# Row numbers for the gathers of a graph network: converted by GpSimd for each slot instead of by ScalarE for eight slots

## The chip, the cores and the metric

The kernel runs on one core of a Trainium2 chip. The metric is device time in microseconds (us) of one execution, as the median of several executions without the profiler. The engines are called as in the profile: PE is TensorE (PEld its weight loads), DVE is VectorE, ACT is ScalarE, POOL is GpSimd and SP is SyncE. POOL issues the indirect DMAs that gather rows; ACT and SP issue plain DMAs.

## The reference

Three rounds of message passing over a graph with 6250 nodes of 512 features (float32) and 100,000 edges that come sorted by target:

```python
x = _layernorm(x + gcn(x, edges) + t_emb @ Wt + bt)        # L = 0
h = relu(mean_of_sources(x) @ Wl1.T + x @ Wr1.T + b1)      # L = 1
y = mean_of_sources(h) @ Wl2.T + h @ Wr2.T + b2            # L = 2
out = _layernorm(x + y)
```

In each round the source rows of all edges are gathered and summed by target. The targets are drawn as 6250·u² with u even between 0 and 1, so targets with low numbers have many edges and those with high numbers few.

## The kernel before, in words

Edges are cut into groups of 256 (CH = 2 gathers of 128 rows). A group fills one of SLOTS = 8 slots of the tile `raw`; eight groups are a block, and each of the three layers (L = 0, 1, 2) goes over the same 42 blocks, so 336 slots and 672 gathers a layer, 1008 slots and 2016 gathers in all.

**GpSimd** does nothing in the layers but these gathers (`gather`, lines 549 to 561, called for two blocks by `two_blocks`, 563 to 566, in the loop of line 568). For each slot n it waits until PE has read the slot (`slot_read[n]`, line 554), counts `slot_claimed` (555) and issues two indirect DMAs (558), each of which takes 128 row numbers (int32, one column of `idx_ring`) and fetches 128 rows of 2 KB. Between two layers it waits until the table for the next one is stored (545, 547).

**The row numbers** lie as int16 in `idx_tab` and are wanted as int32. `idx_ring` holds the numbers of two blocks, 16 columns each. ACT converts them, a block at a time: `next_indices` (1021 to 1025) copies 128 x 16 numbers into one half of the ring and counts `idx_copied`. It does so for the first two blocks ahead of the layers (1032, 1033), and then at the end of each block of its own loop for the block after the next, once the last slot of its block has landed (1158, 1159). POOL waits for `idx_copied` once a block (551).

**PE** waits for a slot (`slot_full[n]`, 1423) and adds its rows to the sum of a window of 64 targets with a one-hot matrix (`add_chunk`, 1330); the first of these matmuls frees the slot before it (1425, 1428). Where a window of targets ends, PE does more (`window_end`, 1285): it closes the sum (1335), adds what belongs to the next window (1304), transposes the sum of a finished tile (1315) and multiplies it by a weight matrix (`weigh`, 1324). In L = 1 and L = 2 it also multiplies the nodes' own rows by a second matrix (`own_rows`, 1345; line 1341); a plan made at the start spreads these over the first part of the layer. **DVE** makes the one-hot matrices and adds up, **ACT** evacuates sums from PSUM.

The order on each engine is that of its own program; semaphores are all that joins them. POOL runs up to eight slots ahead of PE.

Of the kernel before, what the change touches and what calls it, by code (L numbers as in the profile page):

```python
# [5 lines left out]
def gnn_resnorm(nc, x, src, dst, t_emb, w0, b0, wt, bt, wl1t, wr1t, b1, wl2t, wr2t, b2, out):  # L6
    fp32, bf16 = mybir.dt.float32, mybir.dt.bfloat16
    i32, i16 = mybir.dt.int32, mybir.dt.int16
    ALU, ACT = mybir.AluOpType, mybir.ActivationFunctionType
# [14 lines left out]
    CH = 2  # L24
    GROUP = CH * P
    SLOTS = 8
# [57 lines left out]
    with ctx:  # L84
        def sb(name, shape, dt, scope=ctx):
            return scope.enter_context(nc.sbuf_tensor(name, shape, dt))
# [4 lines left out]
        def sem(name):  # L91
            return ctx.enter_context(nc.semaphore(name))
# [10 lines left out]
        idx_tab = sb("idx_tab", [P, (NBLK + 2) * SLOTS * CH], i16)  # L103
# [29 lines left out]
        idx_ring = sb("idx_ring", [P, 2 * SLOTS * CH], i32)  # L133
# [124 lines left out]
        S = {n: sem(n) for n in names}  # L258
        slot_full = [sem(f"slot_full{n}") for n in range(SLOTS)]
# [10 lines left out]
        def free_again(n, L, uses):  # L270

            return L * (n == SLOTS - 1) + 1 + uses
# [9 lines left out]
        def first_block(eng):  # L282

            eng.wait_ge(S["start_made"], 1)
            return eng.value_load(start_blk[0:1, 0:1], min_val=0, max_val=B0MAX)

        def each_block(eng, b0, L, part, step=1):

            begin = (NBLK - b0) * L
            with eng.Fori(begin & BLOCK_BITS, begin + (NBLK - b0), step) as i:  # L290
                part(i, nc.s_assert_within(i + (b0 - begin), 0, NBLK - 1,
                                           skip_runtime_bounds_check_because="the blocks from the first one on"))
# [18 lines left out]
        def own_loads(L):  # L311

            return (0, OWN0, OWN0 + T + 1, OWN0 + 2 * T + 3)[L]
# [166 lines left out]
        def _(pool):  # L480
# [54 lines left out]
            b0 = first_block(pool)  # L535
            pool.wait_ge(S["b0_all_ps"], 1)
            pool.wait_ge(S["ranges_made"], 1)
            pool.wait_ge(S["tabs_made"], 2)
            for L in range(NL):
                if L == 0:  # L540

                    pool.wait_ge(S["stage_stored0"], 16 * 4 * PAIRS)
                    pool.wait_ge(S["stage_stored1"], 16 * 3 * PAIRS)
                elif L == 1:
                    pool.wait_ge(S["x_stored"], 16 * T)
                else:
                    pool.wait_ge(S["h_stored"], 16 * (T + HID + LAG))

                def gather(i, half):

                    pool.wait_ge(S["idx_copied"], i + 1)
                    for n in range(SLOTS):

                        pool.wait_ge(slot_read[n], i + free_again(n, L, 0))
                        pool.sem_inc(S["slot_claimed"], 1)
                        for j in range(CH):
                            at = (half * SLOTS + n) * CH + j
                            nc.gpsimd.indirect_dma_start(  # L558
                                out=raw[:, n, j, :], out_offset=None, in_=tables[L][:, :],
                                in_offset=bass.IndirectOffsetOnAxis(ap=idx_ring[:, at:at + 1], axis=0),  # L560
                            ).then_inc(slot_full[n], 16)

                def two_blocks(i, b):

                    gather(i, 0)
                    gather(i + 1, 1)

                each_block(pool, b0, L, two_blocks, 2)

# [412 lines left out]
        def _(act):  # L982
            a = nc.scalar
# [23 lines left out]
            for n, (first, many) in enumerate(TWOS):  # L1007
                b = first // BT
# [7 lines left out]
            b0 = first_block(act)  # L1016
# [1 line left out]
                         ACT.Copy).then_inc(S["tabs_made"], 1)  # L1018
            act.wait_ge(S["tabs_made"], 3)

            def next_indices(to_half, of_block):

                a.activation(idx_ring[:, bass.ds(to_half * (SLOTS * CH), SLOTS * CH)],
                             idx_tab[:, bass.ds(of_block * (SLOTS * CH), SLOTS * CH)],
                             ACT.Copy).then_inc(S["idx_copied"], 1)

            def next_counts(t1):

                a.activation(cbuf[:, :], counts[:, :, :].rearrange("p t n -> p (t n)")[:, bass.ds(t1 * P - P, P)], ACT.Copy,
                             scale=1.0).then_inc(S["cbuf_ready"], 1)  # L1030

            for blk in range(2):
                next_indices(blk, b0 + blk)

            def take_counts(w, of):

                act.wait_ge(S["c_ready"], w + 1)
                of_nodes = of[:, 0:KEYS].rearrange("p (n h) -> p h n", n=NODE)
                a.activation(counts[:, 0:T - 1, bass.ds(w * NODE, NODE)], of_nodes[:, 1:T, :], ACT.Copy)
                a.activation(counts[:, T - 1:T, bass.ds(w * NODE, NODE)], of_nodes[:, 0:1, :],  # L1040
                             ACT.Copy).then_inc(S["c_taken"], 1)
# [6 lines left out]
            def first_counts():  # L1048

                act.wait_ge(S["c_taken"], DW + 2)  # L1050
                next_tile(1)

            def tile_ahead(done):

                act.wait_ge(S["dense_done"], done)
                next_tile(nc.s_assert_within(done + 1, 1, OWN0, skip_runtime_bounds_check_because="a tile or an empty one"))
# [60 lines left out]
            for L in range(NL):  # L1117

                if L == 1:
                    act.wait_ge(S["x_stored"], 16 * T)  # L1120
                elif L == 2:
                    act.wait_ge(S["h_stored"], 16 * (T + HID + LAG))
                if L > 0:
                    act.dma_start(selfbuf[:, :], rows32[L - 1][2 * P:3 * P, :]).then_inc(S["self_loaded"], 16)

                def counts_of_half(i, half):

                    def taken(i):

                        take_counts(i * 2 + half, (root_ps, dense_ps)[half])  # L1130
                        if half == 1:
                            with act.If(i > COUNT_BLOCKS - 2):
                                first_counts()
                            act.nop()

                    def ahead(d):

                        if half == 0:
                            tile_ahead(d * 2 + 1)
                        else:  # L1140
                            with act.If(d < DENSE_BLOCKS - 1):
                                tile_ahead(d * 2 + 2)
                            act.nop()

                    early_blocks(act, i, taken, ahead)

                def groups(i, b):

                    ends = halves_before(mybir.EngineType.Activation, b)
                    if L > 0:  # L1150
                        rounds = rooted_before(mybir.EngineType.Activation, b)
                    for half in range(2):
                        if L > 0:
                            each(act, rounds[half], rounds[half + 1], lambda r: own_rows(L, r), T)
                        else:
                            counts_of_half(i, half)
                        each(act, ends[half], ends[half + 1], lambda w1: window_end(L, w1))
                    act.wait_ge(slot_full[SLOTS - 1], i * (16 * CH) + 16 * CH)
                    next_indices(i & 1, b + 2)

                each_block(act, b0, L, groups)
                take_transposed(L, T)
                if L == 1:
                    act.wait_ge(S["root_ready"], T + 1)
                    act.dma_start(W[1][:, :, :], wr2t.rearrange("(k p) d -> p k d", p=P)).then_inc(S["wr_loaded"], 16)
                    act.wait_ge(S["root_added"], T + 1 + LAG)
                    act.dma_start(b_all[:, :], b2.rearrange("(a d) -> a d", a=1).to_broadcast([P, D])
                                  ).then_inc(S["b_loaded"], 16)
                    act.wait_ge(S["h_stored"], 16 * (1 + HID + LAG))
                    act.wait_ge(S["self_loaded"], 16 * own_loads(2))  # L1170
                    act.dma_start(selfbuf[:, :], rows32[1][P:2 * P, :]).then_inc(S["self_loaded"], 16)
                    next_counts(1)
                    rectify(L, T - 1)
                    rectify(L, T)
                    take_own(2)
                else:
                    deviation(L, T - 1)
                    deviation(L, T)
                    if L == 0:
                        act.wait_ge(S["dense_done"], OWN0)  # L1180
                        next_counts(1)
                        take_own(1)
# [284 lines left out]
```

## Time and profile before, and how to read them

| what | value |
|---|---|
| median of 3 runs without the profiler | 2886.89 us (2882.86 to 2890.46) |
| profiled execution: span from its first to its last instruction | 3459.0 us |
| profiled execution: time around the span | not shown by the page |
| mean granted TensorE clock in it | 0.902 of full speed |

One execution was traced; it took 572 us more than the median. A row such as "L558 POOL DMA_INDIRECT raw<-rows,idx_ring x1344 | 1277.9, 951 | 939.8 <-issue 498.3" says: line 558, engine POOL, operation, tile written and tiles read, 1344 instructions, together 1277.9 us busy, 951 ns for one; the engine sat idle 939.8 us just before them, and 498.3 us of that ended for no reason that the profile shows ("issue"). "remote" is a release whose source is not in the records. For an indirect DMA on POOL the row tells of the engine's own work, not of the arrival of the rows.

### The profile page before, as it was taken

What the parts mean: (1) busy time and instruction counts of PE and PEld (TensorE: products, weight loads), DVE (VectorE), ACT (ScalarE), POOL (GpSimd) and SP (SyncE); (2) the same over time, 40 slices, a digit from 0 to 9 for tenths busy, and PEclk for the clock granted to TensorE, in tenths of its full rate; (3) what the DMA queues carried; (4) which work ended last, traced back from release to release, by engine and by line L of the source; (5) the groups of instructions that cost most, each with busy time, mean ns of one, the idle gap of its engine ahead of it and who ended that gap; (6) DMA issues with size and microseconds to landing.
All of it is one profiled execution on the core that took longest, in us unless ns stands there. A gap on an engine that the chain in (4) does not pass through costs nothing.

```text
span 3459.0 us, 53711 instructions
## 1 busy us (share of the span) xinstructions
PE 2757.7 (80%) x9822; PEld 1016.0 (29%) x9823; DVE 1126.8 (33%) x2467; ACT 552.0 (16%) x1265; POOL 1944.5 (56%) x2041
## 2 busy tenths in 40 slices
PE   7465676777878888888888787887888888887778
PEld 7212222222222233333332222232333332222222
DVE  8532333333334431112222223231222232333334
ACT  0200111111122211111111111121111111111122
POOL 1266666666555535555666665544555666666553
PEclk9877888888998999999999988999999999988899
DMA  4656566666666645666666666656566666666664
GB/s 167 229 157 177 170 184 190 207 202 208 207 203 184 195 153 174 189 187 200 203 208 203 204 205 199 202 177 196 165 184 179 200 201 190 188 189 188 181 182 139
DMA packets 230235, 654.19 MB, mean 189 GB/s; under 512 B 39294, under 2 KB 40912, under 8 KB 230182
## 3 DMA queue, kind: packets, MB, share of 16 engines
q0 software_dynamic: 161280, 528.61, 52.5%
q1 hardware_dynamic: 46356, 84.02, 6.8%
q10 hardware_dynamic: 22578, 41.30, 3.7%
q8 instruction: 10, 0.16, 0.0%
q14 instruction: 11, 0.09, 0.0%
HBM read 602.43 MB, written 52.15 MB: 189 GB/s over the span
## 4 chain that ended last, share of the span: by engine, by line
PE 38%; issue 23%; another core or an unknown queue 19%; DVEq 7%; DVE 6%; ACTq 4%; ACT 2%; DMA 1%; POOL 0%; SPq 0%; POOLq 0%
PE sum_ps L1330 19%; PE prod_ps L1324 7%; PE root_ps L1341 6%; PE dense_ps L1357 2%; DVEq L907 1%; ACT half_sum L1090 1%; DVEq L363 1%; DVE oh L933 1%; PE root_ps L1213 1%; DMA table<-stage 1%; DVE oh_next L912 1%; DVEq L335 1%; PE selfT_ps L1375 1%; PE sum_ps L1335 1%
## 5 line engine op out<-in xcount | busy, mean ns | idle before, releaser
L558 POOL DMA_INDIRECT raw<-rows,idx_ring x1344 | 1277.9, 951 | 939.8 <-issue 498.3
L1330 PE MATMUL sum_ps<-raw,oh 128*64 128x512 f32 x4032 | 1085.6, 666 | 247.5 <-issue 123.7
L558 POOL DMA_INDIRECT raw<-table,idx_ring x672 | 656.8, 977 | 452.5 <-issue 261.1
L1324 PE MATMUL prod_ps<-W_left,aggT 128*128 128x512 f32 x1176 | 571.7, 631 | 40.7 <-issue 29.2
L1330 PEld LDWEIGHTS sum_ps<-raw,oh 128*64 128x64 f32 x4032 | 294.2, 150 | 901.6 <-issue 895.9
L1341 PE MATMUL root_ps<-W_right,selfT 128*128 128x512 f32 x784 | 383.8, 635 | 83.9 <-issue 32.1
L1330 PE MATMUL sum_ps<-raw,oh_next 128*64 128x512 f32 x1176 | 345.1, 667 | 77.3 <-DVE oh_next L912 68.2
L1090 ACT ACTIVATE half_sum<-sum_ps 64x512 f32<-64x512 f32 x294 | 174.4, 593 | 1396.4 <-remote 691.5
L1324 PEld LDWEIGHTS prod_ps<-W_left,aggT 128*128 128x128 f32 x1176 | 225.6, 202 | 273.2 <-issue 272.6
L884 DVE TENSOR_TENSOR agg<-sum_ps,half_sum 64x512 f32<-64x512 f32 x144 | 98.5, 684 | 465.8 <-ACT half_sum L1090 270.4
L1341 PEld LDWEIGHTS root_ps<-W_right,selfT 128*128 128x128 f32 x784 | 148.9, 200 | 311.8 <-issue 253.9
L909 DVE CAST dst_end<-dst_tab 128x2 f32 x294 | 54.5, 186 | 569.6 <-issue 301.2
L875 DVE TENSOR_TENSOR agg<-sum_ps,half_sum 64x512 f32<-64x512 f32 x147 | 100.2, 681 | 331.9 <-remote 166.9
L933 DVE TENSOR_TENSOR oh<-iota_ps,dst_rel 128x512 f32<-128x512 f32 x253 | 172.6, 682 | 61.4 <-PE sum_ps L1330 24.3
L1357 PE MATMUL dense_ps<-selfbuf,cbuf 128*128 128x512 f32 x298 | 165.3, 637 | 32.0 <-issue 25.6
L912 DVE TENSOR_SCALAR oh_next<-iota_row,win_base,dst_end 128x64 f32<-128x64 bf16 x588 | 162.1, 324 | 49.6 <-DVE dst_end L909 16.3
L1096 ACT ACTIVATE selfT<-selfT_ps 128x512 f32<-128x512 f32 x98 | 58.5, 597 | 713.3 <-PE selfT_ps L1375 300.1
L841 DVE TENSOR_TENSOR X<-root_ps,b_all 128x512 f32 x49 | 33.8, 691 | 287.3 <-PE root_ps L1341 127.3
L1315 PE MATMUL aggT_ps<-ident,agg 128*128 128x128 f32 x588 | 101.2, 298 | 32.2 <-issue 11.9
L1330 PEld LDWEIGHTS sum_ps<-raw,oh_next 128*64 128x64 f32 x1176 | 61.2, 142 | 217.5 <-issue 133.4
L1335 PEld LDWEIGHTS sum_ps<-zeros 128*128 128x128 bf16 x297 | 28.6, 96 | 316.3 <-issue 316.3
L848 DVE TENSOR_TENSOR X<-root_ps,X 128x512 f32 x49 | 33.9, 692 | 209.5 <-PE root_ps L1341 101.8
(213 smaller groups left out, 1404.8 us busy)
## 6 DMA issues: line engine op xcount, KB each, us to landing
selfbuf<-rows ACTq DMA_DIRECT2D x101, 256.0 KB
raw<-rows,idx_ring POOLq DMA_INDIRECT x1344
selfbuf<-table ACTq DMA_DIRECT2D x50, 256.0 KB
rows<-X SPq DMA_DIRECT2D x49, 256.0 KB
rows<-hbuf SPq DMA_DIRECT2D x49, 256.0 KB
X<-rows SPq DMA_DIRECT2D x49, 256.0 KB
out<-X SPq DMA_DIRECT2D x48, 256.0 KB
table<-stage SPq DMA_DIRECT2D x21, 512.0 KB, 4.6
```

The costliest lines, as they stand in the source:

```text
L558: nc.gpsimd.indirect_dma_start(out=raw[:, n, j, :], out_offset=None, in_=tables[L][:, :], in_offset=bass.IndirectOffsetOnAxis(ap=idx_ring[ ...
L875: v.tensor_tensor(agg[0:H, :], sum_ps[0:H, 0:D], half_sum[:, :], ALU.add).then_inc(S["agg_ready"], 1)
L884: v.tensor_tensor(agg[H:P, :], sum_ps[0:H, D:2 * D], half_sum[:, :], ALU.add).then_inc(S["agg_ready"], 1)
L912: made = v.tensor_scalar(oh_next[:, j, :], iota_row[:, 0:H], win_base[:, bass.ds(w1, 1)], dst_end[:, j:j + 1], ALU.add, ALU.is_equal)
L933: v.tensor_tensor(oh[:, which * HR:(which + 1) * HR, :, :].rearrange("p n j e -> p (n j) e"), iota_ps[:, 0:H].unsqueeze(1).to_broadcast([P ...
L1090: a.activation(half_sum[:, :], sum_ps[H:P, bank * D:(bank + 1) * D], ACT.Copy).then_inc(S["half_taken"], 1)
L1315: last = nc.tensor.transpose(aggT_ps[:, k * P:(k + 1) * P], agg[:, k * P:(k + 1) * P], ident[:, :])
L1324: last = mm(product(L, t1), aggT[:, k * P:(k + 1) * P], W[0][:, k, :], start=(k == 0), stop=(k == KD - 1))
L1330: return mm(sum_ps[j * H:(j + 1) * H, bank:bank + D], of[:, j, :], raw[:, n, j, :], start=fresh, stop=False, skip_group_check=True)
L1335: return mm(sum_ps[:, bank:bank + 1], zeros[:, :], zeros[:, 0:1], start=False, stop=False, skip_group_check=True)
L1341: last = mm(out_ps, xT[:, k * P:(k + 1) * P], W[n][:, k, :], start=(k == 0), stop=(k == KD - 1))
L1357: return mm(dense_ps[:, :], cbuf[:, :], rows, start=fresh, stop=False, skip_group_check=True)
```

## The change

GpSimd converts the row numbers itself, with one `tensor_copy` of 128 x 2 numbers (int16 to int32) for each slot. It is issued one slot ahead: the copy for slot n + 1 stands before the two gathers of slot n. The wait for `idx_copied` moves into the loop over the slots and asks for the copy of the slot's own numbers, issued a slot earlier. One further copy, for the first slot, stands ahead of the layers, and POOL now waits for the third part of the tables there (`tabs_made`, 3). ACT loses `next_indices`, its two calls ahead of the layers, and at the end of each block the wait for `slot_full[7]` with the copy behind it.

```diff
-            pool.wait_ge(S["tabs_made"], 2)
+            pool.wait_ge(S["tabs_made"], 3)
+
+            def indices_of(to, group):
+
+                at = to % (2 * SLOTS) * CH
+                nc.gpsimd.tensor_copy(idx_ring[:, at:at + CH], idx_tab[:, bass.ds(group * CH, CH)]
+                                      ).then_inc(S["idx_copied"], 1)
+
+            indices_of(0, b0 * SLOTS)
...
-                def gather(i, half):
-
-                    pool.wait_ge(S["idx_copied"], i + 1)
+                def gather(i, b, half):
+
                     for n in range(SLOTS):
 
                         pool.wait_ge(slot_read[n], i + free_again(n, L, 0))
+                        indices_of(half * SLOTS + n + 1, b * SLOTS + (n + 1))
+                        pool.wait_ge(S["idx_copied"], i * SLOTS + (n + 1))
                         pool.sem_inc(S["slot_claimed"], 1)
                         for j in range(CH):
                             at = (half * SLOTS + n) * CH + j
...
-                    gather(i, 0)
-                    gather(i + 1, 1)
+                    gather(i, b, 0)
+                    gather(i + 1, b + 1, 1)
...
-            def next_indices(to_half, of_block):
-
-                a.activation(idx_ring[:, bass.ds(to_half * (SLOTS * CH), SLOTS * CH)],
-                             idx_tab[:, bass.ds(of_block * (SLOTS * CH), SLOTS * CH)],
-                             ACT.Copy).then_inc(S["idx_copied"], 1)
-
...
-            for blk in range(2):
-                next_indices(blk, b0 + blk)
...
-                    act.wait_ge(slot_full[SLOTS - 1], i * (16 * CH) + 16 * CH)
-                    next_indices(i & 1, b + 2)
```

## Rows read from the trace of the kernel before

**Rows 1.** The page: span, and busy time of each engine

```profile
span 3459.0 us, 53711 instructions
PE 2757.7 (80%) x9822; PEld 1016.0 (29%) x9823; DVE 1126.8 (33%) x2467; ACT 552.0 (16%) x1265; POOL 1944.5 (56%) x2041
```

**Rows 2.** Groups of instructions by line, engine POOL

```profile
L558 POOL DMA_INDIRECT raw<-rows,idx_ring x1344 | 1277.9, 951 | 939.8 <-issue 498.3 <-remote 239.2 <-PE sum_ps L1330 202.4
L558 POOL DMA_INDIRECT raw<-table,idx_ring x672 | 656.8, 977 | 452.5 <-issue 261.1 <-remote 112.6 <-PE sum_ps L1330 78.9
```

**Rows 3.** Timeline of POOL in L = 1: start, duration, instruction, [idle before]

```profile
1512.25 0.95 POOL L558 DMA_INDIRECT raw<-rows,idx_ring  x1 [0.30 <-issue]
1513.50 0.95 POOL L558 DMA_INDIRECT raw<-rows,idx_ring  x1 [0.30 <-issue]
1527.20 0.94 POOL L558 DMA_INDIRECT raw<-rows,idx_ring  x1 [12.75 <-PE sum_ps L1330]
```

**Rows 4.** Timeline of ACT and DVE in the same stretch

```profile
1511.10 0.59 ACT L1090 ACTIVATE half_sum<-sum_ps 64x512 f32<-64x512 f32 x1 [7.01 <-remote]
1516.77 0.60 ACT L1064 ACTIVATE aggT<-aggT_ps 128x512 f32<-128x512 f32 x1 [5.07 <-remote]
1516.77 0.68 DVE L875 TENSOR_TENSOR agg<-sum_ps,half_sum 64x512 f32<-64x512 f32 x1 [8.46 <-remote]
```

**Rows 5.** Line 1023: ns min/median/max, first and last start; ACT's idle time before it

```profile
L1023 ACTq FUSED_REGOPS  x253: 5/57/709, 140.8 to 3445.0; - x127
L1023 ACT ACTIVATE idx_ring<-idx_tab x128: 197/215/217, 140.8 to 3445.1; - x126, 128x16 int32 x2
...
  DMA raw<-rows,idx_ring: 1.8, 1
```

**Rows 6.** Windows: stretch, length, busy by engine PE, PEld, DVE, ACT, POOL, clock, DMA

```profile
148.72:1208.00 1059.28, 790.01 (x2678) 256.78 (x2680) 394.92 (x859) 162.81 (x426) 656.81 (x672) 0.85 0.65 191
1208.00:1246.27 38.27, 31.53 (x98) 11.67 (x95) 20.89 (x53) 11.18 (x27) 0.01 (x2) 0.91 0.19 59
1246.27:1588.50 342.23, 294.26 (x954) 115.75 (x952) 57.84 (x108) 42.84 (x95) 193.63 (x205) 0.94 0.63 189
1588.50:2312.35 723.85, 599.42 (x2066) 208.76 (x2067) 192.67 (x441) 115.13 (x227) 442.12 (x468) 0.92 0.68 205
2312.35:2348.63 36.28, 30.89 (x101) 11.52 (x98) 11.79 (x27) 8.79 (x17) 0.00 (x1) 0.93 0.40 128
2348.63:2699.00 350.37, 297.01 (x954) 117.03 (x954) 82.06 (x155) 45.00 (x104) 196.28 (x205) 0.94 0.61 181
2699.00:3425.67 726.67, 597.86 (x2069) 207.53 (x2067) 241.44 (x619) 134.51 (x307) 445.82 (x468) 0.91 0.64 190
3425.67:3459.00 33.33, 26.04 (x90) 9.41 (x86) 16.66 (x47) 10.19 (x24) 0.00 (x1) 0.98 0.18 58
```

**Rows 7.** Timeline: a conversion on ACT, and the first gather of the block it serves

```profile
3268.73 0.21 ACT L1023 ACTIVATE idx_ring<-idx_tab  x1 [0.20 <-issue]
...
3274.65 0.94 POOL L558 DMA_INDIRECT raw<-rows,idx_ring  x1 [0.30 <-issue]
```

**Rows 8.** Timeline of POOL before the layers: its smallest instructions

```profile
9.01 0.09 POOL L496 MEMSET eps<- 128x1 f32 x1
9.04 0.19 POOL L497 MEMSET ident<- 128x128 f32 x1
...
9.51 0.18 POOL L501 TENSOR_SCALAR_AFFINE_SELECT lifted<-lifted 128x1 f32<-128x1 f32 x1
9.63 0.29 POOL L503 TENSOR_SCALAR_AFFINE_SELECT ident<-ident 128x128 f32<-128x128 f32 x1
```

**Rows 9.** The same ops in the groups by line: mean ns of one

```profile
L501 POOL TENSOR_SCALAR_AFFINE_SELECT lifted<-lifted 128x1 f32<-128x1 f32 x1 | 0.2, 185 | 0.1
L496 POOL MEMSET eps<- 128x1 f32 x1 | 0.1, 88 | 0.0
```

**Rows 10.** Timeline in L = 0: gathers beside an op of DVE on SBUF

```profile
249.17 1.36 POOL L558 DMA_INDIRECT raw<-table,idx_ring  x1 [9.56 <-PE sum_ps L1330]
249.63 1.03 DVE L814 SCALAR_TENSOR_TENSOR oh_key<-iota_key,key_base,key 128x784 bf16 x1
```

## The prediction

> **What bounds the kernel now.** I read the page's busy times, then POOL's groups by line, then its timeline, then a table of windows by layer. The busy shares mislead: PE leads with 80% and POOL has 56% [rows 1]. But POOL's share leaves out what each gather costs between its own end and the next start. In a run of gathers that nothing holds up, they start 1.25 us apart: 0.95 busy and 0.30 idle that no wait ends [rows 3]. Over all, a gather is busy for (1277.9 + 656.8) / 2016 = 0.96 us [rows 2], so POOL needs 2016 x (0.96 + 0.30) = 2540 us for the gathers. Add what lies outside: 148.7 us ahead of the first gather, 38.3 and 36.3 us between layers and 33.3 us behind the last one [rows 6], 257 us in all. That gives 2797 us, and the median of the runs without the profiler is 2887 us. If POOL's pace is the same there, POOL is held up in only 90 us of the layers.
>
> The traced execution spans 3459 us [rows 1], 572 us above the median, and the page shows no time around that span. In the trace POOL is held up for much longer: its idle time before gathers is 939.8 + 452.5 = 1392 us [rows 2], less 605 us (2016 x 0.30), less the waits ahead of the three layers (50 us, which lie within the 148.7, and 38 and 36 us), so about 660 us. I take most of this excess as the trace's own. ACT and DVE stand still for 7, 5 and 8 us with no releaser in the records, and both go on at 1516.77 us [rows 4]; a register operation on ACT that takes 57 ns in the middle took 709 ns once [rows 5]. POOL's pace stays 1.25 us in the same stretch [rows 3], so it isn't what the recording stretches. The sum below is therefore made from the traced durations and carried over to the median of 2887 us; of the span of 3459 us the same instructions would be the cause, but more of their cost would fall into the 660 us in which POOL waits there.
>
> Whether POOL or PE bounds a stage is read from the windows [rows 6]. I scale PE's busy time by the granted clock of the stretch, to what it would be at 2.4 GHz, and set it against POOL's count of gathers at its pace:
> - L = 0: PE 790 x 0.85 = 672 us; POOL 672 x 1.28 = 858 us (977 ns and 0.30 [rows 2]). POOL bounds it clearly.
> - L = 1 and 2, first part (own rows): PE 294 x 0.94 = 277 and 297 x 0.94 = 279 us; POOL 205 x 1.25 = 256 us. PE bounds it.
> - L = 1 and 2, the rest: PE 599 x 0.92 = 551 and 598 x 0.91 = 544 us; POOL 468 x 1.25 = 585 us. POOL, by 35 to 41 us.
> The larger of each, 858 + 277 + 279 + 2 x 585 = 2584, and the 257 us outside make 2841 us, 46 us under the median. So the picture holds to 2%.
>
> **The change part by part.** On ACT 128 conversions go, at 215 ns, 27.5 us in all [rows 5], and one wait a block. Nothing waits for them: the conversion for the block whose first gather starts at 3274.65 us ended at 3268.94 us, 5.7 us before it [rows 7], and that is the closest of the 124 blocks that are converted within the layers. ACT itself waited for the slot once, 1.8 us [rows 5]. ACT is 16% busy [rows 1], so the gain is taken as 0. It could be at most the 27.5 us, if each of them delayed an evacuation that PE needs at once.
>
> On POOL 1009 copies of 128 x 2 numbers are added, 1008 of them in line with the gathers, on the engine that is the slower one for most of the time. The trace has no such copy. The nearest row is an instruction that reads and writes one column of 128 partitions, 185 ns [rows 9]. From below the bound is the start-to-start time of two fills, 9.01 to 9.04 us, 0.03 us [rows 8]; a copy can't shorten POOL's own work, since nothing of it is removed there, so the price isn't negative. From above it is the 185 ns with a pause of 0.30 us behind it like that behind a gather [rows 3], 0.485 us. I take 0.185 us, by the row that is like it in size and in reading its input.
>
> The rest is hidden. The new wait for `idx_copied` asks for a copy that stands in POOL's queue ahead of the two gathers of the slot before, so it is over about 2.5 us earlier. Behind it stand the two gathers of the slot, and PE waits for these; after a stall of POOL the copy is long done as well. The register arithmetic for the copy's address is the sequencer's and runs beside the gathers already queued; its cover is 2.5 us of engine work a slot. The wait for `tabs_made` 3 and the first copy stand in the shadow of the table's storing: ACT's first conversion, which comes after the same count, started at 140.8 us [rows 5], and the first gather at 148.7 us [rows 6]. No DMA changes its issuer or its place in a queue, and SP is untouched. DVE and POOL do disturb each other: a gather took 1.36 us beside a DVE operation of 1.03 us [rows 10], and in L = 0 a gather takes 26 ns more than in the other layers [rows 2]. The same on each copy would be 336 x 0.026 = 9 us, left to the range.
>
> The sum: L = 0 has 336 slots, 336 x 0.185 = 62 us, all of it exposed. The first parts of L = 1 and 2 have 102 slots each, POOL rises from 256 to 275 us and stays under PE's 277: 0. The rests have 234 slots each, 468 x 0.185 = 87 us; POOL's lead there is small and the blocks with many window ends are PE's, so I take half, 43 us. Together 105 us on 2887 us: **2992 us, 3.6% slower**. By the lower bound the same sum is 10 + 7 = 17 us, 2904 us. By the upper one it is 163 us in L = 0, 227 us in the rests and 2 x 28 us in the first parts (256 + 49 = 305 against 277), 446 us, 3333 us.
>
> **The rivals.**
> (a) The copy is cheaper, 0.03 to 0.12 us. The column operation at 9.51 us has its successor start at 9.63 [rows 8], so its place in the stream is 0.12 us: 40 us in L = 0 and half of 56 us in the rests, 68 us, 2955 us. For it: small operations on POOL overlap, a fill of 0.09 us lets the next start after 0.03. Against it: gathers don't overlap, and the copy has two columns and changes the type. The Trainium skill ("Perfetto Trace Analysis", section "GPSIMD Engine Instruction") says that a span on GpSimd isn't to be trusted and that start-to-start spacing is the way to time it. By that rule, which the fills here bear out, this rival would be the forecast.
> (b) The copy is dearer, 0.28 to 0.485 us, because it breaks up the stream of gathers and pays their pause of 0.30 us too, or waits for DVE on SBUF. Then it takes 0.28 x 336 + 0.28 x 234 = 160 us, 3047 us, up to 3333 us. Nothing in the trace stands between two gathers, so nothing speaks against it.
> (c) No change, 2887 us: the copy fits into the 0.30 us that POOL idles behind each gather, or without the profiler a gather costs less than in the trace and PE bounds the layers throughout. Against it: the sum of stages meets the median within 2% with POOL's traced pace.
> (d) Faster: ACT's evacuations are what PE waits for at the end of blocks, and the conversion with its wait for the last slot stands ahead of them. It decides if POOL has room for the copies (under (c)) and ACT has none; then the 27.5 us go, 2860 us. Against it: one wait of 1.8 us in 128.
>
> **How the numbers follow.** The forecast, a copy of 0.12 to 0.28 us, has 0.45; (a) 0.20; (b) 0.19; (c) 0.08; (d) 0.08. A measurement here can tell about 0.3% from no change, some 9 us. Slower by more than that: 0.45 + 0.20 + 0.19 = 0.84; within it 0.08; faster 0.08. The range reaches from 2880 us, which holds (c), to 3200 us, which leaves out the dearest part of (b), some 0.08, and (d): 0.16 outside.
>
> **What would show it.** In the profile after there should be a new group on POOL that writes `idx_ring`, 1009 times, of about 0.19 us; the first gathers of two successive slots should start about 2.7 us apart in place of 2.5 where nothing holds POOL up; PE's idle time before line 1330 should grow, in L = 0 above all, and the first parts of L = 1 and 2 should keep their length. ACT's line 1023 should be gone and its other waits unchanged. I am wrong in the price if the spacing of slots grows by less than 0.1 or more than 0.3 us, and in the bound if it grows as said and the time doesn't follow.

## The result, and the profile after

The changed kernel takes 2939.98 us (median of 4 runs) against 2888.68 us before: 51 us more, ratio 1.018 with a 95% interval of 1.017 to 1.0194. It is slower, as forecast, by about half of what was forecast (105 us).

Its profiled execution spans 2933.4 us, that is as long as its runs without the profiler. The kernel before was therefore traced once more (the first of the experiments below), and that trace spans 2888.8 us; the long one of 3459.0 us was one stretched recording. Comparisons below are with the second trace.

Groups by line on POOL, changed kernel; line 543 is the new copy, line 567 the gathers [rows 2]:

```profile
L567 POOL DMA_INDIRECT raw<-rows,idx_ring x1344 | 1290.9, 960 | 323.1 <-issue 215.0 <-POOL idx_ring L543 99.3 <-PE sum_ps L1328 6.3
L567 POOL DMA_INDIRECT raw<-table,idx_ring x672 | 666.0, 991 | 154.2 <-issue 103.6 <-POOL idx_ring L543 49.9
L543 POOL CAST idx_ring<-idx_tab 128x2 int32 x1009 | 212.7, 211 | 162.1 <-PE sum_ps L1328 50.5 <-ACT idx_tab L1026 42.4 <-DMA rows<-X 31.1
```

The copy takes 211 ns on average, near the 185 ns that the prediction took. What it costs is read from POOL's timeline in a stretch that nothing holds up, changed kernel:

```profile
700.21 0.95 POOL L567 DMA_INDIRECT raw<-table,idx_ring  x1 [0.30 <-issue]
701.16 0.19 POOL L543 CAST idx_ring<-idx_tab 128x2 int32 x1
701.51 0.96 POOL L567 DMA_INDIRECT raw<-table,idx_ring  x1 [0.15 <-POOL idx_ring L543]
702.77 0.95 POOL L567 DMA_INDIRECT raw<-table,idx_ring  x1 [0.30 <-issue]
703.73 0.19 POOL L543 CAST idx_ring<-idx_tab 128x2 int32 x1
```

The copy starts at once when a gather ends, and the next gather starts 0.15 us after the copy. From the end of one gather to the start of the next that is 0.35 us (701.16 to 701.51) where a pause of 0.30 us stood before [rows 3]. With some 0.01 us that each of the two gathers takes longer (960 ns on average for a gather from `rows`, 951 in the second trace of the kernel before), a slot takes 2.57 us (701.16 to 703.73) in place of 2.50. Over all slots of a layer the median distance is 2.57 us here, 2.56 us in run 2 below, and 2.50 us before. The net price is about 0.065 us a slot, a third of the copy's own time.

Windows of the same stages in both traces: stretch, length, busy PE, PEld, DVE, ACT, POOL, clock, DMA share, GB/s. The rows are L = 0, then the first part and the rest of L = 1, then of L = 2. First the kernel before, second trace:

```profile
149.95:1014.81 864.86, 746.20 (x2687) 242.35 (x2688) 398.52 (x865) 164.81 (x430) 660.39 (x672) 0.93 0.77 234
1049.74:1348.11 298.37, 281.89 (x953) 111.67 (x954) 58.15 (x108) 42.83 (x96) 193.94 (x205) 0.99 0.72 217
1348.11:1942.17 594.06, 561.79 (x2086) 200.25 (x2086) 198.08 (x446) 116.52 (x229) 442.29 (x467) 0.99 0.80 249
1971.47:2267.66 296.19, 279.79 (x953) 110.64 (x953) 82.42 (x155) 44.76 (x104) 196.29 (x205) 1.00 0.71 214
2267.66:2861.85 594.19, 561.00 (x2090) 199.98 (x2090) 245.57 (x629) 135.55 (x311) 446.06 (x467) 0.99 0.77 232
```

The changed kernel:

```profile
148.89:1044.02 895.13, 755.33 (x2697) 241.55 (x2697) 399.30 (x870) 156.45 (x389) 740.60 (x1007) 0.91 0.76 226
1075.97:1372.97 297.00, 279.78 (x955) 110.67 (x955) 58.29 (x109) 40.93 (x84) 215.80 (x307) 1.00 0.72 217
1372.97:1975.88 602.91, 561.25 (x2090) 198.89 (x2088) 198.17 (x447) 112.42 (x200) 492.11 (x701) 1.00 0.80 246
2005.42:2301.20 295.78, 279.29 (x955) 110.73 (x955) 82.18 (x155) 42.66 (x92) 223.10 (x307) 1.00 0.72 215
2301.20:2906.75 605.55, 563.71 (x2090) 199.64 (x2088) 247.63 (x628) 130.09 (x282) 495.94 (x700) 0.99 0.77 228
```

L = 0 is 30.3 us longer, the first parts are 1.4 and 0.4 us shorter, the rests 8.9 and 11.4 us longer. The first parts take 298 us with 205 gathers, which POOL could issue in 256 us; PE is busy there for 282 us of them. The rests take 594 us, and POOL's pace asks for 585.

The signs that the prediction named for PE came too: its waits at line 1330 (1328 after the change) for gathered rows grew from 56.6 to 88.9 us. Waits, their sum, their number and the longest; first the second trace of the kernel before, then the changed kernel (`table` is the source in L = 0, `rows` in the other layers):

```profile
PE sum_ps L1330 <- DMA raw<-table,idx_ring: 39.2, 32, 2.6
PE sum_ps L1330 <- DMA raw<-rows,idx_ring: 17.4, 21, 1.7
...
PE sum_ps L1328 <- DMA raw<-table,idx_ring: 57.5, 49, 2.7
PE sum_ps L1328 <- DMA raw<-rows,idx_ring: 31.4, 34, 1.6
```

### The profile page after: what moved, and what is told of

It is laid out like the page before. It is cut to its first block, busy times and chain, and to the rows that moved or that the text cites. A ratio compares the mean times of both kernels' runs of the same rounds, so it can differ in the third digit from the quotient of the medians.

```text
span 2933.4 us, 56105 instructions
## 1 busy us (share of the span) xinstructions
PE 2597.3 (89%) x9822; PEld 964.8 (33%) x9823; DVE 1132.7 (39%) x2467; ACT 529.1 (18%) x1137; POOL 2178.4 (74%) x3050
## 4 chain that ended last, share of the span: by engine, by line
POOL 42%; PE 38%; issue 12%; DMA 3%; POOLq 2%; DVE 1%; ACT 1%; DVEq 0%; SPq 0%; ACTq 0%
POOL raw L567 38%; PE sum_ps L1328 15%; PE root_ps L1339 10%; PE prod_ps L1322 6%; POOL idx_ring L543 4%; PE dense_ps L1355 3%; PE root_ps L1211 1%; PE selfT_ps L1373 1%; DMA selfbuf<-rows 1%; DMA table<-stage 1%; PE aggT_ps L1313 1%; POOLq L563 1%; POOLq L543 1%; DMA raw<-rows,idx_ring 1%; DVE oh_hi L619 0%
## 5 line engine op out<-in xcount | busy, mean ns | idle before, releaser
L567 POOL DMA_INDIRECT raw<-rows,idx_ring x1344 | 1290.9, 960 | 323.1 <-issue 215.0
L1328 PE MATMUL sum_ps<-raw,oh 128*64 128x512 f32 x4032 | 1009.5, 619 | 144.3 <-DMA raw<-table,idx_ring 57.5
L567 POOL DMA_INDIRECT raw<-table,idx_ring x672 | 666.0, 991 | 154.2 <-issue 103.6
L1322 PE MATMUL prod_ps<-W_left,aggT 128*128 128x512 f32 x1176 | 551.2, 612 | 16.7 <-issue 11.5
L1328 PEld LDWEIGHTS sum_ps<-raw,oh 128*64 128x64 f32 x4032 | 268.0, 140 | 745.8 <-issue 742.8
L1339 PE MATMUL root_ps<-W_right,selfT 128*128 128x512 f32 x784 | 362.5, 605 | 34.1 <-issue 23.7
L543 POOL CAST idx_ring<-idx_tab 128x2 int32 x1009 | 212.7, 211 | 162.1 <-PE sum_ps L1328 50.5
L1328 PE MATMUL sum_ps<-raw,oh_next 128*64 128x512 f32 x1176 | 320.6, 624 | 1.7 <-DVE oh_next L921 1.7
L1322 PEld LDWEIGHTS prod_ps<-W_left,aggT 128*128 128x128 f32 x1176 | 217.0, 195 | 238.6 <-issue 237.8
L1339 PEld LDWEIGHTS root_ps<-W_right,selfT 128*128 128x128 f32 x784 | 140.9, 189 | 246.6 <-issue 232.6
```

The lines of the kernel that those rows point to most:

```text
L543: nc.gpsimd.tensor_copy(idx_ring[:, at:at + CH], idx_tab[:, bass.ds(group * CH, CH)]).then_inc(S["idx_copied"], 1)
L567: nc.gpsimd.indirect_dma_start(out=raw[:, n, j, :], out_offset=None, in_=tables[L][:, :], in_offset=bass.IndirectOffsetOnAxis(ap=idx_ring[ ...
L1322: last = mm(product(L, t1), aggT[:, k * P:(k + 1) * P], W[0][:, k, :], start=(k == 0), stop=(k == KD - 1))
L1328: return mm(sum_ps[j * H:(j + 1) * H, bank:bank + D], of[:, j, :], raw[:, n, j, :], start=fresh, stop=False, skip_group_check=True)
L1339: last = mm(out_ps, xT[:, k * P:(k + 1) * P], W[n][:, k, :], start=(k == 0), stop=(k == KD - 1))
```

## The experiments

All times are medians; "before" is the kernel before on the same chip, 2886 us in the first four runs and 2887 us in the others.

**1. The kernel before, traced again** (no edit).

> The kernel before, traced once more. Theory (the long stalls in the first trace belong to that one recording): span within 1% of 2889 us, slots 2.50 us apart, no idle stretches of 5 to 8 us on ACT and DVE. Rival (recording always stretches this kernel, and the changed one escapes it): span again above 3300 us.

One run, 2890.59 us; span 2888.8 us. What it has for line 1023 [rows 5]:

```profile
L1023 ACTq FUSED_REGOPS  x253: 46/57/71, 141.9 to 2874.8; - x127
L1023 ACT ACTIVATE idx_ring<-idx_tab x128: 198/215/217, 141.9 to 2874.9; - x126, 128x16 int32 x2
...
  DMA raw<-table,idx_ring: 56.3, 21
  DMA raw<-rows,idx_ring: 10.8, 5
```

The conversion that ends closest to the first gather of its block, in this trace, and that gather:

```profile
2471.93 0.21 ACT L1023 ACTIVATE idx_ring<-idx_tab  x1 [0.20 <-issue]
...
2479.12 0.95 POOL L558 DMA_INDIRECT raw<-rows,idx_ring  x1 [0.30 <-issue]
```

And POOL's timeline:

```profile
1515.53 0.95 POOL L558 DMA_INDIRECT raw<-rows,idx_ring  x1 [0.31 <-issue]
1516.79 0.95 POOL L558 DMA_INDIRECT raw<-rows,idx_ring  x1 [0.30 <-issue]
1518.04 0.95 POOL L558 DMA_INDIRECT raw<-rows,idx_ring  x1 [0.30 <-issue]
```

A register operation never takes over 71 ns here, where the first trace had 709, and POOL's pace is the same 1.25 us. So the prediction was right to carry POOL's pace over and to leave the stalls out. What stretched that recording is open. The theory's third sign was badly chosen: ACT and DVE stand idle for 5 to 8 us, and up to 12.8 us, in this trace as well, mostly until work of PE ends, but none of these waits is put down to "remote". The first trace also hid something: ACT's conversions do wait for the last slot, 26 times and 67 us together, not once.

**2. The copy alone on POOL, ACT unchanged.**

```diff
...
+            def spare_of(to, group):
+                at = to % (2 * SLOTS) * CH
+                nc.gpsimd.tensor_copy(idx_spare[:, at:at + CH], idx_tab[:, bass.ds(group * CH, CH)]
+                                      ).then_inc(S["bias_made"], 1)
...
                         pool.wait_ge(slot_read[n], i + free_again(n, L, 0))
+                        spare_of(half * SLOTS + n + 1, b * SLOTS + (n + 1))
+                        pool.wait_ge(S["bias_made"], i * SLOTS + (n + 1))
...
```

> The kernel before with the POOL copy of 128 x 2 numbers for each slot added, into a tile that nobody reads; ACT keeps its conversions. Theory (the whole loss is POOL's copy, ACT's part is worth nothing): +48 to +54 us over before, the same as the change, and slots 2.57 us apart. Rival (ACT's freed 27 us gave something back in the change): +60 to +80 us.

2939.64 us, +53 us, ratio 1.0183 (1.0169 to 1.0197): the change's own ratio. The copy on POOL is all of the loss, and what the change frees on ACT is worth nothing that can be measured (the interval is about 4 us to either side).

**3. ACT's conversions away.**

```diff
+            pool.wait_ge(S["idx_copied"], 2)
...
-                    pool.wait_ge(S["idx_copied"], i + 1)
...
-                    act.wait_ge(slot_full[SLOTS - 1], i * (16 * CH) + 16 * CH)
-                    next_indices(i & 1, b + 2)
```

> The kernel before without ACT's conversion at the end of each block and without POOL's wait for it once a block; the gathers go on with the row numbers of the first two blocks, so the sums are of other rows. Theory (nothing waits for these conversions): within 5 us of before. Rival (ACT's evacuations stand behind them): 15 to 27 us faster than before.

Ratio 1.0002 (0.9993 to 1.0011). Neither the conversions nor ACT's 67 us of waiting nor POOL's wait once a block lie on the path. This kernel gathers the rows of the first two blocks again and again; run 2, which gathers the right rows, settles the side of ACT from the other end and comes to the same.

**4. A second copy right behind the first.**

```diff
...
                                       ).then_inc(S["idx_copied"], 1)
+                nc.gpsimd.tensor_copy(idx_spare[:, at:at + CH], idx_tab[:, bass.ds(group * CH, CH)]
+                                      ).then_inc(S["bias_made"], 1)
...
                         pool.wait_ge(S["idx_copied"], i * SLOTS + (n + 1))
+                        pool.wait_ge(S["bias_made"], i * SLOTS + (n + 1))
```

> The changed kernel with a second POOL copy of 128 x 2 numbers right behind the first, into a tile that nobody reads. Theory (the first copy is cheap because it lies in the pause of 0.30 us behind a gather, so the second, which finds no pause, costs its full time): slots 2.70 to 2.77 us apart, +100 to +170 us over the changed kernel. Rival (a copy costs 0.065 us of POOL anywhere, small operations overlap): slots 2.63 us apart, +50 to +65 us over the changed kernel.

3030.51 us, +144 us over before, so 91 us more than one copy (run 2). POOL's timeline of this run:

```profile
699.83 0.95 POOL L571 DMA_INDIRECT raw<-table,idx_ring  x1 [0.30 <-issue]
700.78 0.19 POOL L544 CAST idx_ring<-idx_tab 128x2 int32 x1
700.91 0.18 POOL L546 CAST idx_spare<-idx_tab 128x2 int32 x1
701.24 0.96 POOL L571 DMA_INDIRECT raw<-table,idx_ring  x1 [0.15 <-POOL idx_spare L546]
702.51 0.96 POOL L571 DMA_INDIRECT raw<-table,idx_ring  x1 [0.30 <-issue]
```

A slot takes 2.68 us (699.83 to 702.51), 0.11 more than with one copy. The result lies just under the first theory's range and well above its rival's: the second copy costs more than the first (91 us against 53), but not its full 0.18 us, since it starts 0.13 us after the first and overlaps it. The Trainium skill ("Perfetto Trace Analysis", section "GPSIMD Engine Instruction") advises timing GpSimd's instructions by start-to-start spacing rather than by their spans. The trace agrees for the second copy: its spacing of 0.13 us is near the 0.11 us that it costs, and its span of 0.18 is not. Even that spacing is above the net price of the first copy.

**5. Two copies a slot, one ahead of each gather.** This tells whether the place of a copy sets its price.

```diff
-                at = to % (2 * SLOTS) * CH
-                nc.gpsimd.tensor_copy(idx_ring[:, at:at + CH], idx_tab[:, bass.ds(group * CH, CH)]
+                at = to % (2 * SLOTS * CH)
+                nc.gpsimd.tensor_copy(idx_ring[:, at:at + 1], idx_tab[:, bass.ds(group, 1)]
...
-                        indices_of(half * SLOTS + n + 1, b * SLOTS + (n + 1))
-                        pool.wait_ge(S["idx_copied"], i * SLOTS + (n + 1))
-                        pool.sem_inc(S["slot_claimed"], 1)
                         for j in range(CH):
                             at = (half * SLOTS + n) * CH + j
+                            indices_of(at + CH, b * (SLOTS * CH) + ((n + 1) * CH + j))
+                            pool.wait_ge(S["idx_copied"], i * (SLOTS * CH) + (n * CH + j + 1))
+                            pool.sem_inc(S["slot_claimed"], 1)
```

> The changed kernel with the copy cut in two: one column of 128 numbers ahead of each gather, one gather ahead of its use, so two POOL copies a slot, each of them behind a gather. The run with two copies back to back has shown slots 2.68 us apart, 0.11 us more for the second copy. Theory (a copy right behind a gather lies partly in the gather's pause and costs 0.065 us): slots about 2.63 us apart, +95 to +110 us over the kernel before. Rival (the second copy of a slot costs 0.11 us wherever it stands): slots 2.68 us apart, +140 to +150 us over the kernel before.

3002.06 us, ratio 1.0399 (1.0385 to 1.0413), +115 us: a little above the theory's 95 to 110 us, and well under the 144 us of run 4, which has as many copies. Its timeline:

```profile
701.12 0.96 POOL L568 DMA_INDIRECT raw<-table,idx_ring  x1 [0.16 <-POOL idx_ring L543]
702.09 0.20 POOL L543 CAST idx_ring<-idx_tab 128x1 int32 x1
702.43 0.96 POOL L568 DMA_INDIRECT raw<-table,idx_ring  x1 [0.15 <-POOL idx_ring L543]
703.40 0.19 POOL L543 CAST idx_ring<-idx_tab 128x1 int32 x1
703.75 0.96 POOL L568 DMA_INDIRECT raw<-table,idx_ring  x1 [0.15 <-POOL idx_ring L543]
```

A slot takes 2.63 us (701.12 to 703.75), as the theory has it. A copy behind a gather takes the place of most of that gather's pause; a copy behind a copy does not find one. These copies have one column where those of run 4 have two, but they take no less time (211 ns on average, and 211 and 196 ns for the two of run 4), so the place is what differs.

**6. One copy of 128 x 16 on POOL for a block.**

```diff
-                at = to % (2 * SLOTS) * CH
-                nc.gpsimd.tensor_copy(idx_ring[:, at:at + CH], idx_tab[:, bass.ds(group * CH, CH)]
+                nc.gpsimd.tensor_copy(idx_ring[:, to * (SLOTS * CH):(to + 1) * (SLOTS * CH)],
+                                      idx_tab[:, bass.ds(group * (SLOTS * CH), SLOTS * CH)]
                                       ).then_inc(S["idx_copied"], 1)
...
-                        indices_of(half * SLOTS + n + 1, b * SLOTS + (n + 1))
-                        pool.wait_ge(S["idx_copied"], i * SLOTS + (n + 1))
+                        if n == SLOTS - 1:
+                            indices_of(1 - half, b + 1)
+                        if n == 0:
+                            pool.wait_ge(S["idx_copied"], i + 1)
```

> The changed kernel with one POOL copy of 128 x 16 numbers a block (ahead of the gathers of its last slot, for the next block) in place of eight of 128 x 2. Theory (what costs is the number of copies on POOL, 126 in place of 1008): +5 to +15 us over before. Rival (that POOL converts at all, or the wait for it, costs, whatever the number): +30 us or more over before.

2894.61 us, +7 us, ratio 1.0024 (1.0013 to 1.0035), as the theory says. Converting on POOL is nearly free if it is done once for eight slots: what costs is the number of instructions, not the numbers converted. A copy costs 7 / 126 = 0.06 us here and 51 / 1008 = 0.05 us in the change. In all these runs each copy comes with one wait of POOL, so the price is that of the pair; no run has the wait without the copy.

**7. The copy in L = 0 alone.** The edit of run 2, with both new lines in the loop under `if L == 0`.

> The kernel before with the POOL copy for each slot added in the first layer alone, into a tile that nobody reads; ACT keeps its conversions. Theory (all slots of the first layer pay, and some copies wait there for two-input operations of DVE): +26 to +34 us over before, most of the change's 51 us. Rival (every layer pays its third): +15 to +19 us over before.

2914.37 us, +27 us, ratio 1.0101 (1.0086 to 1.0117): more than half of the change's loss in a third of the slots. By the price of 0.065 us it would be 336 x 0.065 = 22 us. The group of the copy in this run, and the window of L = 0 (864.86 us long in the second trace of the kernel before), show the rest:

```profile
L544 POOL CAST idx_spare<-idx_tab 128x2 int32 x337 | 79.1, 235 | 50.0 <-ACT idx_tab L1029 42.6 <-DMA table<-stage 6.3
...
149.01:1044.96 895.95, 754.32 (x2697) 241.91 (x2698) 399.77 (x870) 164.82 (x430) 741.40 (x1007) 0.91 0.75 226
```

The copies take 235 ns on average, where the median of the changed kernel's copies is 198: some are held up beside operations of DVE, as here in the changed kernel (timeline of POOL and DVE):

```profile
213.76 1.03 DVE L823 SCALAR_TENSOR_TENSOR oh_key<-iota_key,key_base,key 128x784 bf16 x1
214.07 0.77 POOL L543 CAST idx_ring<-idx_tab 128x2 int32 x1
...
214.99 0.96 POOL L567 DMA_INDIRECT raw<-table,idx_ring  x1 [0.15 <-POOL idx_ring L543]
```

The copy took 0.77 us and ended with the DVE operation (214.84 and 214.79 us). This is no single case. In the timelines 34 copies of this run and 47 of the changed kernel (27 of them in L = 0) take over 0.25 us, and every one of them ends within 0.1 us of the end of a DVE operation: 25 and 33 of these are two-input operations (SCALAR_TENSOR_TENSOR or TENSOR_TENSOR), the others TENSOR_SCALAR with one input tile, so the theory's "two-input" is too narrow. Over the usual 0.20 us the long copies of L = 0 take 13 us more in this run and 9 us more in the changed kernel. In the changed kernel 22 + 9 = 31 us, and L = 0 is 30.3 us longer there.

**8. Own rows spread further, no copy.** If PE bounds the first parts of L = 1 and 2 and POOL the rests, the kernel before gains when PE's own rows move from the one to the other.

```diff
-    ROUND_HALVES = 62
+    ROUND_HALVES = 67
```

> The kernel before, POOL as it was, with the nodes' own rows spread over 67 half blocks in place of 62, so that PE has less to do in the first part of the layers L = 1 and 2. Theory (PE bounds these first parts and POOL the rest, where PE has room): the first 205 gathers of each of these layers take 5 to 12 us less, 8 to 25 us off the whole. Rival (POOL, or a wait for rows in the queues, bounds these parts too): within 5 us of before.

2870.79 us, 16 us less, ratio 0.995 (0.9936 to 0.9964): faster than either kernel. Windows of this run, the same stages of L = 1 and 2:

```profile
1042.79:1327.95 285.16, 271.72 (x926) 106.65 (x926) 57.00 (x106) 41.00 (x92) 193.91 (x205) 0.99 0.73 225
1327.95:1925.62 597.67, 567.52 (x2114) 203.74 (x2114) 200.29 (x447) 118.22 (x233) 442.04 (x467) 1.00 0.80 249
1954.92:2240.81 285.89, 271.12 (x925) 106.23 (x925) 79.61 (x151) 42.94 (x100) 197.28 (x205) 0.99 0.73 220
2240.81:2839.39 598.58, 569.18 (x2118) 203.89 (x2118) 249.11 (x633) 137.37 (x315) 447.12 (x467) 1.00 0.77 231
```

The first parts fall by 13.2 and 10.3 us, the rests grow by 3.6 and 4.4. PE's busy time falls by about as much (10.2 and 8.7 us) as the first parts shorten, and grows by 5.7 and 8.2 us in the rests. Line 66 of the kernel would allow up to 83 half blocks for these inputs; no run tried more than 67.

## Why the prediction was right or wrong

**What bounds the kernel: right.** POOL's pace of 1.25 us, taken from one stretched trace, held in every trace, and the stage-by-stage choice held too: L = 0 takes 865 us for the 858 worked out for POOL, the rests 594 for 585 (by the prediction's own terms POOL's lead there is 34 to 41 us, where it says 35 to 41). POOL's idle time beyond the pause of 0.30 us, added up from the timeline of the second trace, is 0 us in L = 0, 42 and 38 us in the first parts and 9.5 and 5.9 us in the rests: 96 us in all, where the prediction worked out 90. In the first parts PE bounds, as said: the copies cost nothing there (1.4 and 0.4 us less) and less work for PE shortens them (run 8). The rests are close to balance: added work for PE lengthens them as well, by 3.6 and 4.4 us in run 8. The first parts take 298 and 296 us, though, where 277 and 279 were worked out for PE.

**ACT's part worth nothing: right**, shown by runs 2 and 3. One row on which it rested (one wait of 1.8 us) was a product of the stretched recording: in the second trace ACT waits 67 us there. The other, 5.7 us of lead at the least [rows 7], is 7.0 us in the second trace (run 1) and shows that POOL doesn't wait for ACT; that ACT's own waiting delays nobody either is shown by the two runs.

**The price of the copy: wrong, and the step that failed.** The prediction took 0.185 us "by the row that is like it in size and in reading its input". That is indeed about how long the copy takes (198 ns at the median), but the step added its span to a pause of 0.30 us that it took to be fixed. The gathers' pause is not fixed: behind a copy it is 0.15 us, and the copy itself starts with none. The net price was 0.065 us, about a third of the term. That the measured time still lies between 2880 and 3200 us is no credit to this term: the range was drawn down to 2880 us to hold "no change". Rival (a), 0.03 to 0.12 us, had the size right, and its way of reading (start to start) came nearer, at 2955 us, but not its reason: the second copy of run 4 shows that overlap of small operations alone gives 0.11 us. The point in rival (c), that the copy fits into the 0.30 us idle time, was the better half of the mechanism; it was given no part in the price.

**The exposure: nearly right, in part by luck.** All of L = 0: yes, and with DVE's disturbance on top, which the prediction left to the range at 9 us; the long copies of L = 0 come to 9 us in the changed kernel (run 7). For the rests it took half, a guess from POOL's small lead there. They grew by 8.9 and 11.4 us of 15.2 each (234 x 0.065), two thirds. The timelines show where the other third went: POOL's idle time beyond its pauses fell from 9.5 to 3.3 and from 5.9 to 2.2 us there, so 6.2 and 3.7 us of the copies fell into time in which POOL waited before, and 15.2 less these is 9.0 and 11.5 us. The prediction's sum with the measured price is 22 + 15 = 37 us. With DVE's 9 us it is 46, with the rests as measured (20 us in place of 15) 51, and 51 were measured. So the direction and the stages were right, and one term was nearly three times too large.

**What would show it wrong** was named as slots that grow by less than 0.1 us. They grew by 0.065, and it is the price that was wrong.

## What to carry to other kernels

Before adding a small instruction to the engine that bounds a stage, look at what the engine's idle time behind each of its instructions is made of: a pause that the profile gives to no wait may be filled by the new instruction, and then only the difference counts. Price it from the nearest pair of instructions of different kinds, start to start. Where the trace has no such pair, "nothing" and "span plus pause" are bounds and no more: here they were 0 and 0.485 us, the span of 0.185 us was nearly three times too much, and the start-to-start time of 0.12 us between two small instructions nearly twice. And count the instructions, not their elements: one conversion of 16 columns for a block cost a seventh of eight conversions of two.

## What was unexpected of the hardware

- A gather on POOL is followed by 0.30 us of idle time if the next instruction is a gather, by none if it is a small copy, and a gather starts 0.15 us after a copy. Why is open. The profile names no wait for the 0.30 us. It puts the 0.15 us down to the copy, though the kernel's own wait there asks only for the copy of a slot earlier.
- A single profiled execution spanned 3459.0 us, with stalls of 5 to 8 us on ACT and DVE whose releaser isn't in the records, while another of the same kernel spanned 2888.8 us. A profiled span that is 20% over the median of the runs was a reason to trace again before reading waits from it.
- The copies on POOL usually took 0.20 us. All 81 that took over 0.25 us, in two traces, ended within 0.1 us of the end of an operation of DVE (run 7).
